# Cross-attention over 32 batches: the K projection and two thirds of the score maxima moved forward by half a batch

## What is computed

```
qh = (q @ Wq.T + bq).reshape(bs, -1, H, DK).transpose(0, 2, 1, 3)
kh = (k @ Wk.T + bk).reshape(bs, -1, H, DK).transpose(0, 2, 1, 3)
vh = (v @ Wv.T + bv).reshape(bs, -1, H, DK).transpose(0, 2, 1, 3)
scores = jnp.einsum('bhqd,bhkd->bhqk', qh, kh) / math.sqrt(DK)
attn = jax.nn.softmax(scores, axis=-1)
out = jnp.einsum('bhqk,bhkd->bhqd', attn, vh)
```

## Time and profile before

| | us |
|---|---|
| runs | 886.71, 887.83, 887.88 (median 887.83) |
| profiled execution | 889.02 |
| its span, first to last instruction | 887.2 |
| TensorE matmuls busy | 825.6 (93%) |
| VectorE busy | 692.8 (78%) |
| ScalarE busy | 559.0 (63%) |
| GpSimd busy | 294.3 (33%) |
| mean granted TensorE clock | 0.974 |

### The profile page before, as it was taken

The page is one execution under the profiler, slowest core; times in us unless marked ns, Lnnn a source line. Parts: engine busy times, 40 slices in busy tenths (PEclk is TensorE's granted clock), DMA queues, the critical chain, the costliest instruction groups (busy, mean ns, idle before and its releaser), DMA issues.

```text
span 887.2 us, 28853 instructions
## 1 busy us (share of the span) xinstructions
PE 825.6 (93%) x11074; PEld 534.8 (60%) x11074; DVE 692.8 (78%) x1245; ACT 559.0 (63%) x759; POOL 294.3 (33%) x170
## 2 busy tenths in 40 slices
PE   6788669999999999999999999999999999998884
PEld 3555426666666666666666666666666666666553
DVE  7767687778787878787878787878787878788498
ACT  4566517666666666666666666666666666666863
POOL 6010524333333333333333333333333333300263
PEclk9989959999999999999999999999999999999898
DMA  6000044333333333333333333333333332222001
GB/s 201 1 10 21 21 129 105 92 86 90 86 87 87 86 88 87 87 86 88 85 87 88 86 86 88 87 87 89 85 92 82 93 84 78 52 53 55 1 1 42
DMA packets 29864, 67.37 MB, mean 76 GB/s; under 512 B 8072, under 2 KB 13192, under 8 KB 29704
## 3 DMA queue, kind: packets, MB, share of 16 engines
q1 hardware_dynamic: 29832, 66.94, 28.7%
HBM read 27.50 MB, written 0.92 MB: 32 GB/s over the span
## 4 chain that ended last, share of the span: by engine, by line
PE 73%; DVE 15%; ACT 5%; issue 5%; DMA 1%; DVEq 0%; POOL 0%; ACTq 0%
PE psum L807 19%; PE psum L846 16%; PE psum L831 14%; PE psum L800 6%; PE psum L794 6%; DVE r_sb L1112 5%; PE psum L851 4%; ACT kh L594 2%; PE psum L722 2%; DVE kl L1091 2%; PE psum L820 2%; PE psum L708 1%; DVE k_stack L1226 1%; DVE rden L1025 1%; DVE mx L1098 1%
## 5 line engine op out<-in xcount | busy, mean ns | idle before, releaser
L1098 DVE TENSOR_REDUCE mx<-psum 128x1 f32<-128x500 f32 x672 | 413.0, 672 | 52.7 <-PE psum L807 49.5
L576 ACT ACTIVATE probs<-psum 125x896 f32<-125x896 f32 x384 | 352.7, 919 | 149.9 <-PE psum L831 146.4
L807 PE MATMUL psum<-kh,q_max 128*128 128x500 f16 x672 | 234.5, 383 | 7.3 <-DVE mx L1098 2.0
L831 PE MATMUL psum<-q_diag,k_stack 97*128 97x224 f16 x1536 | 212.9, 261 | 2.7 <-DMA q_diag<-mT 1.8
L846 PE MATMUL psum<-probs,v_ext 125*32 125x168 f32 x3072 | 189.3, 319 | 1.2 <-ACT probs L576 1.2
L831 PEld LDWEIGHTS psum<-q_diag,k_stack 97*128 97x128 f16 x1536 | 140.7, 98 | 46.6 <-issue 16.9
L442 POOL CAST c_hl<-c_in 128x1500 f16<-128x1500 f32 x32 | 45.9, 1434 | 267.8 <-PE psum L800 261.9
L1091 DVE SCALAR_TENSOR_TENSOR kl<-psum,pack,kh 128x500 f16<-128x500 f32 x96 | 68.0, 735 | 83.4 <-ACT kh L594 83.4
L846 PEld LDWEIGHTS psum<-probs,v_ext 125*32 125x32 f32 x3072 | 60.6, 108 | 114.9 <-issue 97.2
L450 POOL TENSOR_TENSOR q_diag<-q_stack,pack 96x896 f16<-96x896 f32 (+1 forms) x32 | 54.2, 1693 | 171.0 <-PE psum L831 158.7
L851 PE MATMUL psum<-probs,v_ext 125*16 125x56 f32 x3072 | 108.4, 213 | 0.0
(11 more groups left out here) (143 smaller groups left out, 735.0 us busy)
## 6 DMA issues: line engine op xcount, KB each, us to landing
c_in<-ctx_in SPq DMA_DIRECT2D x32, 750.0 KB, 4.3
k_stack<-kh SPq DMA_DIRECT2D x256, 93.8 KB, 2.2
k_stack<-kl SPq DMA_DIRECT2D x128, 93.8 KB, 2.2
pack<-pack_in SPq DMA_DIRECT2D x1, 1107.0 KB, 5.9
q_stack<-qh SPq DMA_DIRECT2D x32, 32.0 KB, 1.8
out<-x_all SPq DMA_DIRECT2D x8, 112.0 KB
pack<-pack_in SPq DMA_DIRECT2D x1, 848.5 KB, 4.7
x_all<-x_in SPq DMA_DIRECT2D x2, 336.0 KB
```

What stands on the lines that cost most here:

```text
L576: nc.scalar.activation(probs[0:KP, t % PBUF, :].rearrange("p (a c) -> p a c", a=2), scores[t % 2][0:KP, :, 0:2 * GC], ACT.Exp, scale=SCALE ...
L807: last = nc.tensor.matmul(bank[:, 0:CH], q_max[u][:, r * P:(r + 1) * P], kh[:, c * CH:(c + 1) * CH], start=True, stop=True)
L831: last = nc.tensor.matmul(scores[t % 2][:, g // 2, (g % 2) * GC:(g % 2 + 1) * GC], k_stack[u][0:ROWS, g, t * KP:t * KP + P], q_diag[u][0:R ...
L1098: dve.tensor_reduce(mx[:, i:i + 1], bank[:, 0:CH], AX.X, ALU.max).then_inc(mx_done, 1)
```

## The change

- K moves from behind step 11 into steps 2, 4 and 6 of the same batch (still for batch b + 2). `kh` and `kl` get two buffers, and a K waits for the M and the stack transfers of the batch two before it, whose buffer it takes.
- The M of a batch are split. The first 14 (`M2`) are made in steps 6 to 11 of the batch two before it, behind its K; the last 7 (`M1`) in steps 0 to 5 of the batch before it. M now run through one third of the context after the other (`M_ORDER`).
- X moves from step 11 to step 7, R from 0 to 2, V from 0, 2, 4 to 1, 3, 5, Y from 6 to 8. The values product of step 11 stands in step 0 of the next batch, behind its first two M, and `o_copy` behind their reduces.
- On VectorE a K copy stands behind the reduce of the next M (`split_late`).
- The slots count from 0 in an even batch and from 1 in an odd one (`U1_SHIFT`). Batch 0 makes all 21 M of batch 1 in steps 0 to 5 (`FIRST_COUNTS`) and 14 of batch 2.
- `stack_k` on SyncE also waits for the stack before it.

```diff
-M_COUNTS = (2, 2, 3, 2, 3, 2, 3, 2, 2)
-V_STEPS, Y_STEP = (0, 2, 4), 6
-X_STEP = 11
-TAIL = [("K", c) for c in range(KC)]
+EARLY_M = 14
+U1_SHIFT = 1
+M_ORDER = [(r, c) for c in range(KC) for r in range(MB)]
+PLAN = ((("M1", "M1"), ()), (("V",), ("M1",)), (("R", "M1"), ("K",)), (("M1",), ("V",)),
...
+FIRST_COUNTS = (3, 3, 3, 3, 2)
...
-        kh, kl = sb("kh", [P, S], F16), sb("kl", [P, S], F16)
+        kh = [sb(f"kh{i}", [P, S], F16) for i in range(2)]
+        kl = [sb(f"kl{i}", [P, S], F16) for i in range(2)]
...
                     sp.wait_ge(kl_done, (n + 1) * KC)
                     settle(sp, sp_settled)
+                    wait_past(sp, k_stacked, n * 192)
+                    settle(sp, sp_settled)
...
                     if i == 0:
-                        wait_past(act, ready["M"], n * NM)
-                        wait_past(act, k_stacked, n * 192)
+                        wait_past(act, ready["M"], (n - 1) * NM)
+                        wait_past(act, k_stacked, (n - 1) * 192)
...
-                        for kind, i in plans[u][t][:half]:
+                        for kind, i in plans[u, first][t][0]:
                             go(kind, i)
+                        if t == 0 and before:
+                            pv(b - 1, KT - 1, 1 - u)
                         if t >= lag:
                             pv(b, t - lag, u)
-                        for kind, i in plans[u][t][half:]:
+                        for kind, i in plans[u, first][t][1]:
                             go(kind, i)
...
+                                if kind == "M2" and s1:
+                                    m_max(b + 2, i, bank)
+                                    split_late()
...
+                                if kind == "K" and s1:
+                                    late.append(i)
+                            if t == 0 and part == 0 and before and s2:
+                                o_copy(b - 1, 1 - u)
```

More of the change, by code:

```diff
@@ new lines, with unit_plan @@
+U1_SHIFT = 1
+M_ORDER = [(r, c) for c in range(KC) for r in range(MB)]
+PLAN = ((("M1", "M1"), ()), (("V",), ("M1",)), (("R", "M1"), ("K",)), (("M1",), ("V",)),
+        (("M1",), ("K",)), (("M1",), ("V",)), (("K",), ("M2",)), (("M2",), ("X", "M2")),
+        (("Y", "M2"), ("M2", "M2")), (("M2", "M2"), ("M2",)), (("M2",), ("M2",)), (("M2", "M2"), ("M2",)))
+FIRST_COUNTS = (3, 3, 3, 3, 2)
+def unit_plan(u, first=False):
+    made = {"M1": 0 if first else EARLY_M}
+    steps = []
+    for t, parts in enumerate(PLAN):
+        step = []
+        for part in range(2):
+            kinds = list(parts[part])
+            if first and part == 0 and t < len(FIRST_COUNTS):
+                kinds += ["M1"] * FIRST_COUNTS[t]
+            units = []
+            for kind in kinds:
+                if kind == "Y" and u:
+                    continue
+                units.append((kind, made.get(kind, 0)))
+                made[kind] = made.get(kind, 0) + 1
+            step.append(units)
+        steps.append(step)
+    assert made["M1"] == NM and made["M2"] == EARLY_M and made["V"] == made["K"] == KC
+    return steps
@@ L125, in ring_slots, with active @@
+def active(kind, s1, s2, before):
+    return {"K": s1, "M2": s1, "R": before, "Y": before}.get(kind, s2)
 def ring_slots():
[L127 to L132, removed]
+    rounds = {}
+    for u, first in ((0, False), (1, False), (0, True)):
+        rounds[u, first] = [unit for step in unit_plan(u, first) for part in step for unit in part]
+    return {key: {unit: (k + key[0] * U1_SHIFT) % RING for k, unit in enumerate(units)}
+            for key, units in rounds.items()}
@@ L135, in early_bank, with left_in_ring @@
+def left_in_ring(slots, u, first, s1, s2, before):
+    left = {}
+    for (kind, i), slot in slots[u, first].items():
+        if active(kind, s1, s2, before):
+            left[slot] = (kind, i)
+    return left
 def early_bank(kind, i):
@@ L854, in pv, with of_batch, body @@
                     last.then_inc(pv_done, 1)
[L856 to L862 removed]
+                def of_batch(kind, b, pair):
+                    return {"K": b + 2, "M2": b + 2, "R": b - 1, "Y": pair - 1}.get(kind, b + 1)
+                def body(b, pair, u, s1, s2, before, held):
+                    first = not before
+                    held = dict(held)
                     def go(kind, i):
[L865 to L868 removed]
+                        if active(kind, s1, s2, before):
+                            n, slot = of_batch(kind, b, pair), slots[u, first][kind, i]
+                            unit(kind, i, n, u if kind in ("K", "M2") else 1 - u, ring[slot], held[slot])
                             held[slot] = (kind, i, n)
@@ L922, in early @@
                         bank = early_bank(kind, i)
-                        unit(kind[0], i, n, n, banks[bank], held[bank])
-                        held[bank] = (kind[0], i, n)
+                        unit({"K1": "K", "M": "M1"}.get(kind, kind), i, n, n, banks[bank], held[bank])
+                        held[bank] = ({"K1": "K", "M": "M1"}.get(kind, kind), i, n)
                 held = [None] * 8
```

157 lines of the change are left out of this document (73 added, 84 removed).

## The result

The changed kernel takes 912.6 us (median of 4 runs, 909.66 to 912.93) against 887.4 for the kernel before (4 runs, 886.71 to 887.88). The ratio is 1.0264, its 95% interval 1.0241 to 1.0287: 2.6% slower. The forecast was 904, its range 882 to 915. The profiled execution took 909.66 with a span of 907.9, 20.7 more than before; the other three are some 3 us longer, their mean granted clock is 0.970 to 0.974 where the profiled one has 0.978, and they left no trace that would show where it goes. In what follows "a pair" is the distance of two batches in the loop.

The account below looks back on a forecast made before the run. TensorE, with only 1.16 us of waits per pair, was taken to bound the kernel. Middle +11.8, head +7.0 and tail -2.4 gave +16.4 us on the profiled 889.02, so 905.4; the median, 1.2 lower, 904, range 882 to 915.

Parts of the forecast that it names:

- 1.16 us of waits: Middle of the loop: TensorE's waits per pair of batches before the change; removing them could win at most 16 us.
- X waits for the third K copy: Step 7, every batch: X waits 0.35 to 0.37 us for the third K's bank, costing 0.74 per pair.
- The odd start: Start of odd batches: first M 0.18 us late, second 0.37, behind a row of reduces; 0.55 per pair.
- The chain through R: Steps 3 and 4: V waits 0.05 us and an M 0.18, 0.23 per batch where it was 0.43.
- Step 9: One M in step 9 waits 0.09 us in each batch, 0.18 per pair.
- The wait for the copy of O: Step 1: the values product waits 0.07 us for the copy of O, now behind two reduces.
- The turn of the loop: Loop turn on TensorE: between 0 and 0.6 us per pair, taken as 0; 0.6 kept for the range (+8 us).
- The boundary wait goes: Start of each batch: the score's 0.17 us wait for the maxima row disappears, gaining 0.34 per pair.
- The floor: Middle: the matmuls of a pair take 43.12 us in any order that waits for nothing.
- The head: Batches 0 and 1: +5.8 us, mainly from the count of reduces, and +1.2; together +7.0.
- The tail: Batch 30 takes 18.1 us, batch 31's first exponential starts at +21.6 instead of 24.03; -2.4 us.
- The clock: Middle: granted clock stays at 1.00; the rival that it falls gave some 970 us, chance 0.02.

Follow-up runs that it names:

- e2: Changed kernel with the third K copy cut to 50 of 500 columns in the loop: 897.26 us, ratio 1.0077 to the kernel before.
- e9: Changed kernel with the third K copy put ahead of the next reduce on VectorE: 913.34 us, ratio 1.0262 to the kernel before.
- e10: e9 with K and V also exchanged between steps 5 and 6: 895.78 us, ratio 1.0075 to the kernel before.
- e1: Changed kernel with an empty place for Y counted in odd batches, so all batches start on the same slot: 906.53 us, ratio 1.0203 to before.
- e3: Changed kernel with each maximum reduced over 250 of 500 columns: 875.48 us, ratio 0.9863 to the kernel before.
- e6: Kernel before, with maxima copied out ahead of exponential 11 and the last values product behind the second K: 888.16 us, ratio 0.9988.
- e12: Changed kernel with the three K copies of batch 0 alone put ahead of the next reduce: 909.11 us in one run.
- e7: Kernel before, with one M moved from step 1 to step 2: 880.85 us, ratio 0.9907.

## Why the prediction was right, and where not

The direction and, in the middle, the mechanism hold: TensorE has little to win from an order beyond its 1.16 us of waits, and the new order makes VectorE late at other places. In the head the number holds and its cause does not. By its steps:

- **X waits for the third K copy.** Right in place and cause (e2, e9, e10), mis-sized: 0.37 forecast, 0.47 measured. X started 1.80 after the first early M (424.34 to 426.14), as worked out. But TensorE would be there 0.10 earlier than I had it: I took the way out of the values product from its pitch to an M, 0.52, and to X it is 0.42 (e2). The wait is 0.20 per pair larger than forecast.
- **The odd start**: 0.55 forecast, 0.52 measured, and the even batch waits for nothing there. Right; e1 removes most of it.
- **The chain through R**: 0.23 per batch forecast, 0.31 measured (0.15 at V, which was to be 0.05, and 0.16 at M). **Step 9**: 0.09 forecast, 0.14 measured. Both right in kind; together +0.26 per pair. The wait for the copy of O in step 1 of the even batch is 0.05 for 0.07.
- **The turn of the loop** was taken at 0. It costs 0.11 to 0.13 per pair on TensorE, and e3 shows the same (0.11) where almost nothing else waits. This is the one term that was put at nothing and costs something. Its range of 0.6 was too wide.
- **The boundary wait goes**: yes, a score opens the batch 0.22 behind an M. The e6 run adds what the forecast did not say: in the kernel before that wait was worth nothing, since the reciprocal behind it was late too.
- **The floor.** The waits listed make .94 + .52 + .62 + .28 + .12 + .05 = 2.53 per pair, and 45.52 - 2.53 = 42.99, with 42.95 from e3. The forecast's floor is 43.12, for "any order that waits for nothing". It is some 0.15 too high, since two units cost TensorE less where they now stand: R is followed by M after 0.46 (438.19 to 438.65) where V followed it after 0.51 (332.93 to 333.44), and X adds 0.42 + 0.15 - 0.52 = 0.05 between a values product and an M where it added 0.08 between a score and a values product (0.49 + 0.07 in step 11 for 0.48 in step 10). So the miss of 0.40 per pair is .20 (X) + .26 + .12 (turn) less .03 (odd start), .02 (step 1) and some .13 (floor).
- **The head**, +7.1 for +7.0. Its working comes out in the trace of after: the reduces begin 2.39 behind the start of batch 0 (134.42, forecast 2.36), the 21st starts 14.68 later (149.10, forecast 11.8 + 0.66 + 2.1 = 14.56), and steps 6 to 11 take 10.32 for 10.25. But the 11.8, the count of reduces, is not the cause in all of it. They follow each other without a break only up to the 13th, through step 2; behind it TensorE waits for K copies (1.21 in step 3), and with reduces of 0.42 instead of 0.68 steps 2 to 5 are only 0.5 shorter (e3). That the sum came out is in part luck. In e3 batch 0 as a whole was even 28.56 long (126.11 to 154.67), but its reduces began 0.5 later behind its start, at 129.00, and the granted clock was 0.76 from 130 to 137, so that number decides nothing about steps 0 and 1. Another place of the K copies on VectorE takes only 0.10 off step 3 (e12). What sets steps 3 to 5 stays open.
- **The tail**: batch 30 took 18.10 for 18.1, the exponential +21.53 for +21.6. Right.
- **The clock.** It stayed at 1.00 through batches 2 to 30, with 2.5 us of waits in every 45.5. The Trainium skill (TensorE: Matmul & The Clock Gate, section "A second HAM failure mode: psum-queue depth-cycling") describes a kernel that cycles through PSUM banks and whose clock swings for its frequent short idles between groups of matmuls; it gives no length for them. The trace of this kernel, with single waits of up to 0.47, shows no such swing.

The median lies 8.6 above the forecast of 904: 4.3 are in the spans (5.5 of the middle, less 1.0 of an earlier start and 0.3 behind). The other 4.3 lie in the profiled runs: the forecast took 1.2 off because that of before was above its median, and that of after is 2.9 below its own. Neither difference was traced.

## What to carry to other kernels

Where a ring of banks couples two engines, work out for each moved unit which bank it takes, whose read gives that bank back, and what stands before that read on the reading engine; the total load of that engine (here 76 to 78%) says neither that there are waits nor where. To take a read out of a full row helps (e10), and so does moving the unit that meets the row (e7); to change places within the row moves the wait to the neighbour (e9, e12), and to remove a wait in front of another one wins nothing (e6). And bound the gain first: the waits of the old order were 1.16 us in 44.28, and the head, with 35 maxima in batch 0, cost 7 of the 16 us that could be won in the loop.

## What was not expected of the hardware

- The same values product is followed by X (a transpose, fp16, 128 columns) after 0.42 and by an M (fp16, 500 columns) after 0.52. It is not the number of columns: V, with fp16 matmuls of 128 columns, follows it after 0.52 too (340.63 to 341.15 in the trace of before).
- A queued K copy holds VectorE for 0.64 to the next start (425.36 to 426.00) though it lasts 0.73, and X's matmul began 0.05 after its end. The values product, which waits for bank O, starts 0.24 after the end of the copy of O.
- TensorE idled 2.77 us for ScalarE at 840 to 843, with a granted clock of 0.91 from 838 to 856; before, an idle of 1.63 was followed by 0.80. The longer idle came with less loss of clock. Why it did is open.
